# Cross-attention scores as float32r pairs in 64-row tiles, with PSUM banks dealt out anew

## The reference

```python
q = (x @ Wq).reshape(b, n, N_HEADS, HEAD_DIM)
k, v = jnp.split(ctx @ Wkv, 2, axis=-1)
...
q = apply_axial_rope(q, pos_map)
k = apply_axial_rope(k, ctx_pos_map)
scale = 1.0 / np.sqrt(HEAD_DIM).astype(np.float32)
logits = jnp.einsum('bqhd,bkhd->bhqk', q, k) * scale
w = jax.nn.softmax(logits, axis=-1)
attn = jnp.einsum('bhqk,bkhd->bqhd', w, v)
attn = attn.reshape(b, n, N_HEADS * HEAD_DIM)
return attn @ Wout + bout
```

## Time and profile before

| | us |
|---|---|
| median of 3 runs | 3319.63 |
| lowest, highest | 3304.61, 3321.81 |
| the profiled execution, its own time | 3316.54 |
| its span in the trace | 3314.8 |
| TensorE busy | 2716.1 (82%) |
| VectorE busy | 1958.6 (59%) |
| ScalarE busy | 1433.1 (43%) |
| GpSimd busy | 1177.7 (36%) |

### The profile page before, as it was taken

One profiled execution on the slowest core, in us unless ns is written; L12 is line 12 of the kernel. 1 busy time (PEld: TensorE's weight loads), 2 busy tenths in 40 slices (PEclk: granted clock), 3 DMA queues, 4 the chain that ended last, 5 costly groups with the idle time before them and its releaser, 6 DMA issues.

```text
span 3314.8 us, 50665 instructions
## 1 busy us (share of the span) xinstructions
PE 2716.1 (82%) x20138; PEld 1454.0 (44%) x20154; DVE 1958.6 (59%) x3064; ACT 1433.1 (43%) x2577; POOL 1177.7 (36%) x1118
## 2 busy tenths in 40 slices
PE   5788888876677676589988898888768989899787
PEld 3565656553223232268845444444433333333244
DVE  3323232333689889956526566656655657476477
ACT  3232333320545555423426262635315546465555
POOL 0443333441566666600023625243243424241000
PEclk8888888887888888799998999998879989899999
DMA  2222222130330304032332424243155435252301
GB/s 87 71 59 62 52 78 60 47 87 14 121 116 13 127 26 140 13 140 95 137 108 86 128 90 125 93 122 130 39 117 107 105 69 112 61 109 53 118 26 39
DMA packets 209370, 280.04 MB, mean 84 GB/s; under 512 B 84640, under 2 KB 111680, under 8 KB 208240
## 3 DMA queue, kind: packets, MB, share of 16 engines
q1 hardware_dynamic: 209136, 276.81, 29.4%
HBM read 192.08 MB, written 59.12 MB: 76 GB/s over the span
## 4 chain that ended last, share of the span: by engine, by line
PE 39%; DVE 10%; issue 5%; ACT 4%; POOL 2%; DMA 1%; SPq 0%; ACTq 0%; DVEq 0%; POOLq 0%
PE ps L236 7%; PE ps L3368 4%; PE ps L1846 4%; PE ps L1857 4%; PE ps L3355 4%; PE ps L3341 3%; PE ps L3300 3%; PE ps L3332 2%; PE ps L2512 1%; ACT arena L3446 1%; PE ps L2520 1%; DVE arena L2775 1%; DVE arena L1434 1%; DMA arena<-arena 1%; DVE arena L2773 1%
## 5 line engine op out<-in xcount | busy, mean ns | idle before, releaser
L236 PE MATMUL ps<-arena 128*128 128x512 f32 (+3 forms) x1280 | 473.6, 522 | 18.3 <-ACT arena L2612 6.1
L3545 DVE TENSOR_REDUCE arena<-ps 128x1 f32<-128x512 f32 x512 | 330.3, 685 | 229.2 <-PE ps L3341 227.8
L3446 ACT ACTIVATE arena<-ps 128x512 f32<-128x512 f32 x512 | 287.8, 597 | 283.2 <-PE ps L3355 279.7
L1466 POOL TENSOR_TENSOR arena<-arena 128x1024 f32<-128x1024 f32 x128 | 311.0, 2430 | 192.9 <-DVE arena L1458 192.9
L1482 PE MATMUL ps<-arena 128*128 128x512 f32 x512 | 267.2, 662 | 55.8 <-POOL arena L1466 55.5
L1458 DVE TENSOR_TENSOR_SCAN arena<-ps,arena 128x1024 f32<-128x1024 f32 x128 | 291.5, 2278 | 32.9 <-ACT ps L1449 32.9
L236 PEld LDWEIGHTS ps<-arena 128*128 128x128 f32 (+2 forms) x1296 | 193.2, 154 | 252.3 <-issue 172.9
L1449 ACT ACTIVATE ps<-arena 128x511 f32<-128x511 f32 x256 | 165.1, 679 | 188.3 <-DVE arena L1458 188.1
L576 POOL TENSOR_TENSOR arena<-arena 128x31 f32<-128x31 f32 (+15 forms) x217 | 130.1, 600 | 324.2 <-DMA arena<-d_a 307.8
L3355 PE MATMUL ps<-arena 99*128 99x512 bf16 x512 | 198.4, 390 | 45.3 <-ACT arena L3446 33.4
L3341 PE MATMUL ps<-arena 96*128 96x512 bf16 x512 | 201.4, 395 | 19.1 <-issue 15.4
(11 more groups left out here) (352 smaller groups left out, 5254.1 us busy)
## 6 DMA issues: line engine op xcount, KB each, us to landing
arena<-d_bc SPq DMA_DIRECT2D x32, 1024.0 KB, 5.7
arena<-d_x SPq DMA_DIRECT2D x24, 1024.0 KB, 6.8
arena<-d_parts SPq DMA_DIRECT2D x192, 128.0 KB, 4.6
d_x<-arena SPq DMA_DIRECT2D x64, 256.0 KB, 2.5
arena<-arena SPq DMA_DIRECT2D x128, 128.0 KB, 2.1
arena<-in_D_wlm SPq DMA_DIRECT2D x12, 1024.0 KB, 6.6
d_parts<-arena SPq DMA_DIRECT2D x32, 384.0 KB, 2.4
d_signs<-arena SPq DMA_DIRECT2D x32, 256.0 KB, 2.1
```

Source lines behind the costliest of these rows:

```text
L236: ins = pe.e.matmul(ps[:m, :n], lhsT(k), rhs(k), start=(k == 0), stop=(k == chunks - 1))
L1466: pool.e.tensor_tensor(h, h, s.bc[:, turn % s.SLOTS, 1], ALU.mult).then_inc(*pool.up("scan_hC"))
L3446: act.e.activation(s.E[:, k % 2, j], s.rexp.bank((u, i)), ACT.Exp).then_inc(*s.rexp.empty(act, (u, i)))
L3545: dve.e.tensor_reduce(s.mx[:, u % 2, t, h:h + 1], s.rmax.bank((u, m)), AX.X, ALU.max, negate=True).then_inc(*s.rmax.empty(dve, (u, m)))
```

## The change

1. Scores. The rotated q and k are cut into two float32r parts instead of three bf16 (one cast and one subtract fewer). A head's stack is three 16-row blocks instead of six, 48 rows, so two heads fit above each other: even heads on partitions 0 to 47, odd heads on 64 to 111. A step pair issues two score matmuls, one per 64-row tile, into two PSUM banks. The maximum rides on two more rows (48, 49 of each tile) in two float32r parts; the rows of ones against it are written by two DMAs at the start. The parts' transposition is fp32.
2. Order on TensorE: two exponentials' scores, two maxima's scores, values, small work, where it was one and one.
3. PSUM: exponentials have banks 0 to 2, maxima 3 to 5, values 6, small work bank 7 alone.
4. `misc` places small work anew: xT at steps 9, 13, 23, 25; y in pairs, at 27 and 29 and at 9 and 11 of the next unit (then aT at 13); after the last unit at 13, 15, 17, 19. The norm of the batch moves from steps 2 and 4 to 18 and 20.
5. Buffers of the stage are placed as tensors of their own (`PLACED`).

```diff
-    Q_PARTS = (0, 1, 0, 2, 1, 0)
-    K_PARTS = (0, 0, 1, 0, 1, 2)
-    N = 6 * 16
+    Q_PARTS = (0, 0, 1)
+    K_PARTS = (0, 1, 0)
+    N = 3 * 16
...
-        s.Qs, s.Ks = carve(s.SLOTS, s.HU, L, dt=BF16), carve(s.SLOTS, s.HU, L, dt=BF16)
+        s.Qs, s.Ks = carve(s.SLOTS, s.HU // 2, L, dt=F32R), carve(s.SLOTS, s.HU // 2, L, dt=F32R)
...
-        s.ring = Ring("cross", ps, 6, 2, [(name, s.EMPTIES[name[0]]) for i in s.iterations() for _, name in s.misc(i)])
-        s.rexp = Ring("cross_exp", ps, 0, 2, [((u, e), "act") for u in range(s.UNITS) for e in range(s.STEPS)])
-        s.rmax = Ring("cross_max", ps, 2, 3, [((u, m), "dve") for u in range(s.UNITS) for m in range(s.STEPS)])
-        s.rav = Ring("cross_av", ps, 5, 1, [((u, g), "act") for u in range(s.UNITS) for g in range(2)])
+        s.ring = Ring("cross", ps, 7, 1, [(name, s.EMPTIES[name[0]]) for i in s.iterations() for _, name in s.misc(i)])
+        s.rexp = Ring("cross_exp", ps, 0, 3, [((u, e), "act") for u in range(s.UNITS) for e in range(s.STEPS)])
+        s.rmax = Ring("cross_max", ps, 3, 3, [((u, m), "dve") for u in range(s.UNITS) for m in range(s.STEPS)])
+        s.rav = Ring("cross_av", ps, 6, 1, [((u, g), "act") for u in range(s.UNITS) for g in range(2)])
...
+            items += [(1, ("Rq", f)), (7, ("Rk", f))]
...
+            items += [(3, ("mT", i, 1)), (21, ("turn", i, 0))]
...
+            items += [(5, ("turn", i - 1, 1)), (13 if i > C and i % C == 1 else 11, ("aT", i - 1))]
...
+            items += [(at, ("xT", nb, t)) for t, at in enumerate((9, 13, 23, 25))]
+        ends = range(T) if i == s.UNITS else (0, 1) if i > 0 and i % C == 0 else (2, 3) if i > C and i % C == 1 else ()
+        at = (13, 15, 17, 19) if i == s.UNITS else (27, 29, 9, 11)
+        items += [(at[t], ("y", i // C - 1, t)) for t in ends]
...
         for a, part in enumerate((s.Q_PARTS, s.K_PARTS)[w]):
-            sp.e.dma_start(dst[16 * a:16 * a + 16], d[:, :, part, :].rearrange("h d l -> d h l")).then_inc(*sp.up(f"cross_stack_{'qk'[w]}", 16))
+            for p in range(2):
+                at = 64 * p + 16 * a
+                sp.e.dma_start(dst[at:at + 16].bitcast(F32), d[p::2, :, part, :].rearrange("h d l -> d h l")).then_inc(*sp.up(f"cross_stack_{'qk'[w]}", 16))
...
+        hh, p = 2 * g + j // 2, j % 2
+        rows = slice(64 * p, 64 * p + s.N + 2)
+        pe.e.matmul(s.rexp.bank((u, i)), s.Ks[rows, slot, hh, k * P:(k + 1) * P], s.Qs[rows, slot, hh, :],
...
-            for m in range(s.STEPS):
+            for m in range(1, s.STEPS, 2):
                 if s.unit(i) is not None:
+                    s.pe_exp(pe, i, m - 1)
                     s.pe_exp(pe, i, m)
                 if s.unit(i + 1) is not None:
+                    s.pe_max(pe, i + 1, m - 1)
                     s.pe_max(pe, i + 1, m)
...
-                if m in misc:
-                    s.pe_misc(pe, misc[m])
+                for at in (m - 1, m):
+                    if at in misc:
+                        s.pe_misc(pe, misc[at])
```

115 lines of the change are left out of this document (48 added, 67 removed).

## The result

| | before | after |
|---|---|---|
| executions, us | 3304.6, 3319.6, 3319.7, 3321.8 | 3383.1, 3387.2, 3398.4, 8436.8 |
| median of all four | 3319.6 | 3392.8 |
| ratio to before, 95% interval | | 1.022 (1.017 to 1.027) |
| profiled execution, its own time | 3316.5 | 3398.4 |
| TensorE busy in the span | 2716.1 | 2728.3 |

The execution of 8436.8 us is a slow one that nothing here explains, and the ratio leaves it out. By the ratio the change costs 73 us; the median of the three others, 3387.2, lies 68 above before. The forecast, 3273 in 3226 to 3334, missed by 114 to 120 us and on the wrong side.

A forecast was written before the change was run, and what follows sets the result against it. TensorE was taken to set a plain unit. Plain halves -16.2, batch ends -15.4 and -4, rows +8, units 13 and 14 -6.5, unit 15 -6, head -10, tail +3.5: -46.6, so 3273 us, range 3226 to 3334.

The forecast's parts named there:

- I take 0.50: Scores in pairs: a step pair's four score matmuls take 0.50 us; bounds 0.47 overlapped, 0.93 not, 1.7 with weight loads.
- One bank for small work: Each small work waits until the one before is emptied; with switching, a plain unit takes 32.1 us, a half 16.05 against 17.0.
- TensorE's own sum fell from 32 to about 25: TensorE's work in a plain unit shrinks by 7 us, of which the waits leave 1.9 as gain.
- The walk: Step-by-step paper schedule of one plain unit with a single small-work bank: TensorE stands 1.4 us at mT, 2.1 at Rk.
- Switching tile shape, 0.6 a unit: Six small works a unit now lie between row-tiled scores; changing shape costs 0.6 us a unit, bounds 0 and 1.2.
- 81.4 against 89.1: Batch ends: the 1.5 units there take 81.4 us instead of 89.1, twice, -15.4 in all; a third end gains 4.
- The norm: At batch ends: 2.2 us for the square root's table loads; maxima rows queued behind the stores add 4 each, +8 together.
- The head, -10: Up to the first exponential: 7 us per stack instead of 9.8, gaining 10 us in all, bounds 0 and -15.
- Units 13 and 14, -6.5: Late units without projections: VectorE-bound at 22 us a unit instead of 27.0, -6.5 us.
- unit 15, -6: The last unit, exponentials alone: ScalarE-bound at 19 us instead of 24.9, -6 us.
- The tail, +3.5: At the end, y 1 to 3 each wait for VectorE's add of the one before: +3.5 us.
- B: Rival, chance 0.13: TensorE's clock falls behind the wait at each Rk, 39 us more, time 3312.

The follow-up runs named there:

- b_place: The kernel before with the change's placement of small work and norm alone; scores, order and banks as before: 3297.4 us beside 3318.7.
- b_place1: The kernel before with the change's placement and also its banks (three for exponentials, one for small work): 3352.7 us.
- a_moved: The kernel after with small work at other steps in six plain units, so that nothing follows a turn within two step pairs: 3404.5 us.
- a_norm14: The kernel after with the norm's square root at step 14 instead of 18 and its scaling at 16 instead of 20: 3372.8 us.
- a_old2: The kernel after with the placement and norm steps of before, two banks for small work and two for exponentials: 3340.3 us beside 3318.7.
- a_f32best: The kernel after with two banks each for small work and exponentials, norm at 14 and 16, stores behind the stacks, float32r pairs kept: 3338.1 us.
- a_v23: The kernel after with V moved from step 15 to step 23 in the units in which a batch is normed: 3402.4 us.
- a_onetile: The kernel after with every score matmul in one 64-row tile, odd heads' scores left out, even heads' computed twice: 3475.2 us.
- a_single: The kernel after with TensorE's order as before (exponential, maximum, exponential, maximum): 3394.2 us.
- a_bf16: The kernel after with its two parts and the maxima's rows in bf16 instead of float32r, low bits of the scores left out: 3326.0 us.

## Why the prediction was wrong

The stage's +65.6 splits along one chain of kernels: placement -20.4 (before to b_place), the banks +45.9 (to b_place1), float32r pairs with their order +40.1 (to after). The sizes depend on the order in which the parts are added: placed on two small banks the pairs cost 44.7, on the old placement 17.0. Each step is one run, so a few us of each are noise. Why the pairs cost so much more with the new placement is open; the low clock is a part of it.

- **"I take 0.50"** for a four, bounds 0.47, 0.93 and 1.7. It is 0.67 where both banks are free, and 1.22 in the four shown where they are not. That they overlap was right. The step failed in taking float32r's pace in a large matmul for its pace in a 64-row tile: there one takes 0.28 to 0.34, bf16 0.22, beside weight loads of 0.19 and 0.10. The 0.60 by the Trainium skill's ratio (TensorE: Matmul & The Clock Gate, Part 3) was nearer than mine, still too low. That ratio is for four tiles; two gave 1.13 to 0.67 here, 1.7 times, 0.84 of ideal.
- **One bank for small work, and "TensorE's own sum fell from 32 to about 25".** This is the step that failed most. The walk had the plain unit's waits right, 1.4 and 2.1 against 1.51 and 2.09, but TensorE is busy 32.12 us of a unit, not 25. A unit was to be 32.1 and is 36.7: by the rows 2.7 more for 16 fours, 1.3 for Rk at the low clock, and about 0.6, the rest, in waits for exponential banks (0.2 each). These cannot be had back one by one: without the wait and the low clock at Rk the unit stays at 36.7 (a_moved). The 15 plain halves make +23.7 where -14.3 was put. That is 38 us, the largest single part of the 118 between what was put (-46.6) and what was measured (+71.1, the last column of the table).
- **Switching tile shape, 0.6 a unit.** Near enough. From start to start Rq takes 3.63 instead of 3.54, Rk 1.89 instead of 1.72, V 1.99 instead of 1.78, aT and two turns 0.3 more together: about 0.8 a unit.
- **"81.4 against 89.1"** at batch ends: 94.8 and 93.5. The placement does gain here, 30 us over both with two banks; the single bank takes 28 of them back in bf16, and 35 with the pairs. Of the 13.4 too few at the first end, 6.9 are 1.5 plain units at their measured price. The other 6.5 no run takes apart. TensorE waits 3.60 ahead of mT at the sines (2697.55), but the low clock is a small part: 0.87 over the stretch against 0.89 before, at most some 2.5 us by an estimate.
- **The norm.** Costed as 2.2 for the table loads and 4 for rows in the queue, twice. The wait is 3.18; the rows made TensorE wait once, 1.59; and what was not in the sum, 17 us at half the clock follow at the first norm. Of the +28.5 behind the batch ends 14.7 lie in the two halves right behind a norm, where +6.1 was put; the rest is plain halves. I had moved the norm on paper without asking what TensorE runs after it: at step 4 Rk and V follow, at 18 no projection for half a unit. Whether that is the reason is not shown (a_norm14, b_place).
- **The head, -10.** From SP's round and larger packets I took 7 us per stack. Reads are 768 KB per stack before and after, and the pace stayed 9.87. I had counted the write's bytes and not those. So there is no gain; why the head takes 5.6 more is open, and about as much is what heads of like kernels differ by (5.3).
- **Units 13 and 14, -6.5; unit 15, -6.** Unit 15 takes 23.7, not 19: there four exponentials come every 2.67 us, since TensorE puts values of 1.0 between the pairs and ScalarE waits 0.60 for each next four. Units 13 and 14 meet the third norm at the low clock, 31 us long (22.2 for a half). Their -6.5 does not follow from its own terms either: twice 22 instead of 27 is -10.
- **The tail, +3.5**: +5.5. The second to fourth y wait 0.78 each, 2.3; the first y, at the low clock, takes 5.72 instead of 3.70, 2.0 more.
- **Chances.** B's mechanism was in the profile, priced as a rival on its own with everything else held at the forecast. It is not a rival to the single bank but its consequence, and should have raised the price of each wait. At Rk itself it was small: over the twelve Rk behind a wait of 2.09 the low clock cost 11.6 us, where B put 39.

## What to carry to other kernels

Price a new wait on TensorE twice: the wait, and the work behind it until the clock is back, which here took from 3 to 31 us. Before a stage is called bound by another engine, measure TensorE's own sum again. Before packing matmuls into row tiles, measure one tile's own pace in the data type, and see that the banks of both tiles come free together. A bank given to evacuation is taken from hand-overs: here, moving one from small work to exponentials cost 46 us with the old scores and 41 with the pairs, at batch ends above all, where small works stand close together. If two edits gain and lose at once, try them apart: the placement alone was good for 20 us that the whole change hid.

## What the runs showed that was not expected

- TensorE, 88% or more occupied with float32r scores in 64-row tiles and column-tiled values, stayed at the 1.2 GHz level for 20 to 31 us, twice in after, three times in a_moved, and in all other float32r kernels whose norm stands at step 18. In those with the norm at 2 or 14 (a_old2, a_norm14, a_f32best) no such busy stretch was over 11 us. The end came under Rq (2783.72 in after, 2628.24 in a_moved), 2 us behind V where V was put there (a_v23), once behind a turn (3146.95), while other turns did not end it. In a_onetile, where no two tiles overlap, TensorE stayed there for 51 us without a gap. In the six kernels with scores over 96 rows no such stretch was longer than 7 us. It is no rule that it happens: the same norm wait was followed by 4 us of low clock elsewhere. What decides is open; large float32r matmuls hold full speed in another stage.
- Row tiles run as streams of their own. In a_single the even head's maximum is issued between the two heads' exponential scores. The odd head's exponential score still starts with the even head's (both at 2595.61), and that maximum at 2595.95, behind a matmul that was issued after it.
- A wait of 2.09 us ahead of Rk was followed by the low level in 11 of 12 units of after (from start to start Rk took 2.3 to 3.6 instead of 1.89) and in 9 of 12 of a_bf16; one of 1.66 in b_place1 in 3 of 12.
